# First loads in order of need, products of weights and idle products in TensorE's waits, and a last stage shared over three engines

## The reference

```python
def fp8_gemm_optimized(x, input_scale, kernel, kernel_scale):
    s_in = input_scale[0]
    s_k = kernel_scale[0]
    x_q = (x.astype(jnp.float32) / s_in).astype(jnp.float8_e4m3fn)
    k_q = (kernel.astype(jnp.float32) / s_k).astype(jnp.float8_e4m3fn)
    y = jnp.dot(x_q.astype(jnp.float32), k_q.astype(jnp.float32), preferred_element_type=jnp.float32)
    return y * (s_in * s_k)
...
y = y.astype(dtype) + bias
...
x = _layernorm(x + _L3_ffn_ref(x, L3_ffn_kernel, L3_ffn_input_scale, L3_ffn_kernel_scale, L3_ffn_bias), axis=-1)
```

## Time and profile before

| | |
|---|---|
| median of 3 runs | 1708.81 us (1707.7 to 1712.8) |
| profiled execution | 1693.4 us, span 1691.6 us |
| PE busy | 1276.5 us, 75% of the span |
| DVE busy | 1196.2 us, 71% |
| POOL busy | 811.6 us, 48% |
| ACT busy | 708.3 us, 42% |
| mean granted PE clock | 0.887 |

### The profile page before, as it was taken

One profiled execution on the slowest core, in us unless ns is written; L12 is line 12 of the kernel. 1 busy time (PEld: TensorE's weight loads), 2 busy tenths in 40 slices (PEclk: granted clock), 3 DMA queues, 4 the chain that ended last, 5 costly groups with the idle time before them and its releaser, 6 DMA issues.

```text
span 1691.6 us, 40998 instructions
## 1 busy us (share of the span) xinstructions
PE 1276.5 (75%) x15261; PEld 883.3 (52%) x15261; DVE 1196.2 (71%) x2568; ACT 708.3 (42%) x1453; POOL 811.6 (48%) x1014
## 2 busy tenths in 40 slices
PE   4988868886878868689998786846888742988820
PEld 2555635655645556456665455843555541655510
DVE  3986848994688857578886575435888525997777
ACT  1553425554555544233443353423555420555510
POOL 2553437772376735434552462534566425556610
PEclk9998969998999989789999898877999865999965
DMA  8000000000000000000000000212000102000000
GB/s 326 1 1 1 0 0 1 0 1 22 0 1 0 0 1 13 0 5 1 0 0 1 1 0 26 49 45 106 0 2 0 34 20 21 1 1 1 0 2 25
DMA packets 17814, 29.93 MB, mean 18 GB/s; under 512 B 4211, under 2 KB 14067, under 8 KB 16970
## 3 DMA queue, kind: packets, MB, share of 16 engines
q1 hardware_dynamic: 15818, 24.97, 4.3%
q0 software_dynamic: 1920, 3.94, 1.5%
HBM read 23.91 MB, written 4.98 MB: 17 GB/s over the span
## 4 chain that ended last, share of the span: by engine, by line
PE 40%; DVE 23%; issue 17%; POOL 12%; ACT 5%; DMA 2%; SPq 1%; POOLq 0%; DVEq 0%; ACTq 0%
PE ps L331 31%; DVE maxima L424 6%; PE ps L447 4%; DVE arena L426 4%; PE ps L779 3%; ACT arena L434 2%; DVE heads_out L721 2%; POOL arena L864 2%; POOL arena L511 2%; POOL inv_norm L859 2%; DVE sq_sum L993 1%; POOL rstd L365 1%; POOL arena L1889 1%; DVE gate L1746 1%; POOL arena L2175 1%
## 5 line engine op out<-in xcount | busy, mean ns | idle before, releaser
L331 PE MATMUL ps<-arena 64*64 64x64 f32 (+5 forms) x7937 | 384.7, 280 | 36.2 <-DVE arena L2083 7.0
L331 PEld LDWEIGHTS ps<-arena 64*64 64x64 f32 (+4 forms) x7937 | 238.8, 134 | 166.0 <-issue 121.5
L511 POOL TENSOR_TENSOR arena<-arena,w_const 128x1024 f32<-128x1024 f32 x96 | 182.4, 1901 | 154.8 <-DVE arena L711 68.6
L424 DVE TENSOR_REDUCE maxima<-ps 128x16 f32<-128x1024 f32 (+1 forms) x144 | 158.5, 1101 | 54.6 <-PE ps L331 51.0
L434 ACT ACTIVATE arena<-arena 128x1024 f32<-128x1024 f32 (+1 forms) x144 | 138.5, 962 | 129.3 <-DVE arena L426 128.4
L447 PE MATMUL ps<-w_const,arena 128*128 128x128 f32 x1024 | 145.0, 284 | 50.6 <-ACT arena L434 33.8
L859 POOL TENSOR_TENSOR inv_norm<-sq_floor,minus_half 128x16 f32<-128x16 f32 x32 | 121.9, 3810 | 88.1 <-DVE sq_floor L996 88.0
L426 DVE TENSOR_TENSOR arena<-ps,maxima 128x1024 f32<-128x1024 f32 (+1 forms) x144 | 159.3, 1106 | 4.9
L447 PEld LDWEIGHTS ps<-w_const,arena 128*128 128x128 f32 x1024 | 116.9, 145 | 73.4 <-ACT arena L434 44.0
L441 ACT COPY arena<-ps 128x1024 f32<-128x1024 f32 (+1 forms) x144 | 131.3, 912 | 55.1 <-PE ps L447 55.0
L365 POOL TENSOR_TENSOR rstd<-var_eps,minus_half 128x1 f32<-128x1 f32 x144 | 80.0, 567 | 145.6 <-DVE var_eps L827 101.4
(11 more groups left out here) (296 smaller groups left out, 2663.9 us busy)
## 6 DMA issues: line engine op xcount, KB each, us to landing
experts<-in_pack_moe SPq DMA_DIRECT2D x2, 4180.0 KB, 20.0
w_fa<-in_pack_fa SPq DMA_DIRECT2D x2, 1024.0 KB, 11.8
moe_in<-state SPq DMA_DIRECT2D x2, 1024.0 KB, 5.9
w_a<-in_pack_a SPq DMA_DIRECT2D x1, 1824.0 KB, 16.9
moe_out<-arena SPq DMA_DIRECT2D x5, 256.0 KB, 2.3
w_fg<-in_pack_fg SPq DMA_DIRECT2D x2, 537.0 KB, 12.2
ctxT<-in_ctxT SPq DMA_DIRECT2D x1, 1024.0 KB, 7.8
out<-state SPq DMA_DIRECT2D x1, 1024.0 KB, 5.1
```

Of the source, the lines that this page charges most:

```text
L331: return nc.tensor.matmul(o, lhsT, rhs, start=start, stop=stop, skip_group_check=True)
L424: nc.vector.reduce_max(mx, sc, X_AXIS).then_inc(signal["max_ready"], 1)
L511: nc.gpsimd.tensor_tensor(keys_wide(s).rearrange("p (b h t) -> p b h t", b=SEQS, h=8), key8(s).rearrange("p (b t) -> p b t", b=SEQS).unsqu ...
```

## The change

Six things are done.

- **First loads.** const is cut in a head (identity, causal, own_head, rope8; 328 of 1105 columns) and a rest. SP issues the head, rows, tiles 0 and 1 of x, a0, the other 14 tiles of x, const's rest, and then what came before. DVE's setup makes only what the first stage needs; four tables are made in `late_tables`, behind L0_ATTN. ACT makes one copy of a scratch column before all, and POOL fills the blank values before it waits.
- **Products of weights.** PE makes the biases of a stage, and the chain's 32 products, before it waits for the phase before; the wait until they are kept moves behind the first front. The POOL fill goes behind the first staging.
- **Idle products.** `keep_busy(o, n)` makes n products of 128x512 in bf16 into a bank that nobody reads: 12 before L0_CROSS, 8 and 5 around the chain's wait, 12 before L1_CROSS, 12 and 18 in moe1, 16 before L2_ATTN and before L3_ATTN each (when twelve of the sixteen tiles are done), 12, 10, 10 and 14 in moe2. That is 145.
- **Last stage by three engines.** POOL casts to bf16, adds the bias and the residual and makes the power and the norm's bias. ACT scales the input, squares it, doubles the large values, copies the turned group, scales the output and writes the norm. DVE splits, masks, rounds, takes a row maximum (its way to carry over-range values to NaN) and the statistics. All scratch is double, loops are written out, and the scaling of a later group stands ahead of or behind norms as in the diff.
- **Last stage's loads** are issued after alibi's, long before.
- **Store** of the output by groups, four DMAs of 256 KB.

```diff
+        def keep_busy(o, n):
+            for _ in range(n):
+                mm(o, ident16[:, :], causal16[:, :].unsqueeze(1).broadcast_to([P, 8, S]))
...
-                pool.wait_ge(ctx_loaded, 16)
-                pool.wait_ge(tile_done, 2 + 16 * phases[0])
-                for s in STREAMS:
-                    last = nc.gpsimd.memset(big(s, 4, 8 * 96), 0.0)
-                last.then_inc(values_blank, 1)
+                if phases[0] != L0_ATTN:
+                    pool.wait_ge(ctx_loaded, 16)
+                    pool.wait_ge(tile_done, 2 + 16 * phases[0])
+                def blank_values():
+                    for s in STREAMS:
+                        last = nc.gpsimd.memset(big(s, 4, 8 * 96), 0.0)
+                    last.then_inc(values_blank, 1)
+
+                if phases[0] == L0_ATTN:
+                    blank_values()
...
+                    if front and not middle and front.ph != L0_ATTN:
+                        blank_values()
...
-                pe.wait_ge(tile_done, 2 + 16 * phases[0])
+                bias_bank = bank(1, 3) if phases[0] == L2_ATTN else bank(0, 1)
                 for k, ph in enumerate(phases):
...
-                pe.wait_ge(bias_kept, biases_kept(phases))
+                if phases[0] in (L2_ATTN, L3_ATTN):
+                    pe.wait_ge(tile_done, 2 + 16 * phases[0] - 4)
+                    keep_busy(bank(1, 1) if phases[0] == L2_ATTN else bank(0, 2), 16)
+                elif phases[0] != L0_ATTN:
+                    keep_busy(bank(0, 2), 12)
+                pe.wait_ge(tile_done, 2 + 16 * phases[0])
...
+        def late_tables(dve):
+            dve.wait_ge(const_rest_loaded, 16)
+            dve.wait_ge(loaded["scales"], 16)
+            dve.wait_ge(masks_loaded, 4 * 16)
+            for l in range(2):
+                nc.vector.tensor_tensor(rope_f[l][:, :], part("const", "rope_xpos"),
+                                        weights["scales"][:, l * 256:(l + 1) * 256], ALU.mult)
+            nc.vector.tensor_scalar(own16[:, :], own_u8[:, :], 0.0, OFF, ALU.is_equal, ALU.mult)
...
+                if L0_ATTN in phases:
+                    late_tables(dve)
...
-                pe.wait_ge(tile_done, 2 + 16 * phases[0])
                 for c in range(8):
                     for par in range(2):
                         rows = slice(par * S, (par + 1) * S)
-                        mm(pair(0, 0)[rows, c * D:(c + 1) * D], part("a1", "wv")[rows, c * S:(c + 1) * S],
+                        mm(pair(1, 0)[rows, c * D:(c + 1) * D], part("a1", "wv")[rows, c * S:(c + 1) * S],
                            part("a1", "wo")[rows, c * D:(c + 1) * D])
                 for n, ph in enumerate(GLU):
-                    last = mm(bank(1, 0, n * D, (n + 1) * D), ones_row[:, :], part("rows", glu_pack(ph) + "_b2"))
+                    last = mm(bank(1, 2, n * D, (n + 1) * D), ones_row[:, :], part("rows", glu_pack(ph) + "_b2"))
                 last.then_inc(vo_made, 1)
+                keep_busy(bank(0, 2), 8)
+                pe.wait_ge(tile_done, 2 + 16 * phases[0])
+                keep_busy(bank(0, 2), 5)
                 pe.wait_ge(vo_kept, 1)
                 by_tile_steps(pe, chain_steps(f_tensor(pe), glu_tensor(pe), l1_tensor(pe), phases))
             return run
...
+                keep_busy(bank(0, 2), 12)
...
+            keep_busy(bank(1, 1), 12)
...
+            keep_busy(bank(1, 1), 18)
...
         def fp8_pool(ph):
-            with pool_engine.Fori(0, GROUPS) as g:
-                group_norm_pool(pool_engine, 2, g)
+            pool = pool_engine
+            def bf16_input(g):
+                pool.wait_ge(tile_done, 2 + 16 * (ph - 1) + 4 * (g + 1))
+                if g >= 2:
+                    pool.wait_ge(fs["f_in"], 2 * (g - 2) + 2)
+                nc.gpsimd.tensor_copy(fp[g % 2]["x16"], group_of(state, g)).then_inc(fs["f_x16"], 1)
+
+            for g in range(3):
+                bf16_input(g)
+            for g in range(GROUPS):
+                f = fp[g % 2]
+                pool.wait_ge(fs["f_y16"], g + 1)
+                nc.gpsimd.tensor_tensor(f["sum16"].rearrange("p (t d) -> p t d", t=4),
+                                        f["y16"].rearrange("p (t d) -> p t d", t=4),
+                                        bias8.unsqueeze(1).broadcast_to([P, 4, D]), ALU.add).then_inc(fs["f_biased"], 1)
+                pool.wait_ge(fs["f_biased"], g + 1)
+                if g >= 2:
+                    pool.wait_ge(tile_done, 2 + 16 * ph + 4 * (g - 1))
+                nc.gpsimd.tensor_tensor(f["acc"], group_of(state, g), f["sum16"], ALU.add).then_inc(gs["g_sum"], 1)
+                if g == 0:
+                    bf16_input(3)
+                pool.wait_ge(gs["g_var"], USES + g + 1)
+                nc.gpsimd.tensor_tensor(f["rstd"], f["var"], minus_half[:, 0:4], ALU.pow).then_inc(gs["g_rstd"], 1)
+                pool.wait_ge(gs["g_rstd"], USES + g + 1)
+                nc.gpsimd.tensor_tensor(f["bias"], f["minus_mean"], f["rstd"], ALU.mult).then_inc(fs["f_bias"], 1)
 
         def fp8_tensor(ph):
             pe = tensor_engine
-            turned = ps[0][:, 0, :].bitcast(BF16)
-            with pe.Fori(0, GROUPS) as g:
-                pe.wait_ge(fs["f_rounded"], g + 1)
+            for g in range(GROUPS):
+                f, turned = fp[g % 2], ps[g % 2][:, 0, :].bitcast(BF16)
...
+            def scaled_input(g):
+                f = fp[g % 2]
+                act.wait_ge(fs["f_x16"], g + 1)
+                if g >= 2:
+                    act.wait_ge(fs["f_max"], 2 * (g - 2) + 1)
+                    act.nop(nofuse=True)
+                nc.scalar.activation(f["x"], f["x16"], ACT.Identity, bias=zero8, scale=inv8[:, 0:1])\
+                    .then_inc(fs["f_in"], 1)
+                nc.scalar.activation(f["size"], f["x16"], ACT.Square, bias=zero8, scale=inv8[:, 0:1])\
+                    .then_inc(fs["f_in"], 1)
...
+            for g in range(GROUPS):
+                turned_copy(g)
+                if g == 0:
+                    large_values(1)
+                scaled_output(g)
+                if g >= 1:
+                    normal(g - 1)
+                if g + 2 < GROUPS:
+                    scaled_input(g + 2)
+                if 1 <= g < GROUPS - 1:
+                    large_values(g + 1)
+            normal(GROUPS - 1)
...
+            def round_group(g):
+                f = fp[g % 2]
+                dve.wait_ge(fs["f_in"], 2 * g + 1)
+                half, small = split(f["x"], f["half8"], f["small8"])
+                half.then_inc(fs["f_halved"], 1)
+                small.then_inc(fs["f_masked"], 1)
+                dve.wait_ge(fs["f_in"], 2 * g + 2)
+                nc.vector.tensor_scalar(f["mask"], f["size"], SMALL, None, ALU.is_ge)
+                dve.wait_ge(fs["f_masked"], 2 * g + 1)
+                dve.nop(nofuse=True)
+                if g >= 2:
+                    dve.wait_ge(fs["f_turned"], g - 1)
+                nc.vector.tensor_copy(f["q_x"], f["small8"]).then_inc(fs["f_masked"], 1)
+                nc.vector.reduce_max(f["largest"], f["size"].rearrange("p (t d) -> p t d", t=4), X_AXIS)\
+                    .then_inc(fs["f_max"], 1)
+                dve.wait_ge(fs["f_large"], g + 1)
+                dve.wait_ge(fs["f_masked"], 2 * g + 2)
+                nc.vector.copy_predicated(f["q_x"], f["mask"], f["large"]).then_inc(fs["f_rounded"], 1)
+                dve.wait_ge(fs["f_max"], 2 * g + 1)
+                nc.vector.tensor_scalar(f["over"], f["largest"], OVER, 3e38, ALU.is_gt, ALU.mult)\
+                    .then_inc(fs["f_max"], 1)
+                dve.wait_ge(fs["f_max"], 2 * g + 2)
...
+            head = sum(packs["const"][1][n][1] for n in ("ident", "causal", "own_head", "rope8"))
+            x_tiles = dram["x"].rearrange("(t p) d -> p t d", p=P)
+            sp.dma_start(weights["const"][:, 0:head], packs["const"][0][:, 0:head]).then_inc(loaded["const"], 16)
+            sp.dma_start(weights["rows"][:, :], packs["rows"][0]).then_inc(loaded["rows"], 16)
+            sp.dma_start(state[:, 0:2, :], x_tiles[:, 0:2, :]).then_inc(x_loaded, 16)
             sp.dma_start(weights["a0"][:, :], packs["a0"][0]).then_inc(loaded["a0"], 16)
-            sp.dma_start(state[:, :, :], dram["x"].rearrange("(t p) d -> p t d", p=P)).then_inc(x_loaded, 16)
-            sp.dma_start(weights["rows"][:, :], packs["rows"][0]).then_inc(loaded["rows"], 16)
+            sp.dma_start(state[:, 2:TILES, :], x_tiles[:, 2:TILES, :]).then_inc(x_rest_loaded, 16)
+            sp.dma_start(weights["const"][:, head:], packs["const"][0][:, head:]).then_inc(const_rest_loaded, 16)
             sp.dma_start(weights["scales"][:, :], packs["scales"][0][0].partition_broadcast(P))\
                 .then_inc(loaded["scales"], 16)
 
...
-            sp.wait_ge(tile_done, 2 + 16 * PHASES)
-            sp.dma_start(out.rearrange("(t p) d -> p t d", p=P), state[:, :, :]).then_inc(out_stored, 16)
-            sp.wait_ge(out_stored, 16)
+
```

(7 more changed lines are left out.)

257 lines of the change are left out of this document (147 added, 110 removed).

## The result

The changed kernel takes 1640.23 us (median of 4 runs, 1635.91 to 1646.56) against 1710.8 (median of 4) for the kernel before beside it: ratio 0.9595, 95% interval 0.956 to 0.963, 70.6 us less. The forecast was 1638 in a range of 1623 to 1662.

The account below looks back on a forecast made before the run. No engine holds the whole span (wait chain: PE 40%, DVE 23%, issue 17%). Terms 15.0 + 11.7 + 15.7 + 1.8 − 2.0 + 28.5 = 70.7 us off 1708.8 give 1638.1 us, range 1623 to 1662.

Parts of the forecast that it names:

- Start, 15.0: Start of the kernel: reordered loads and setup bring the first projection from 23.76 to about 8.7 us, saving 15.0 us.
- Rival C: Start: the slow 4.09 us issue of the rows load now delays the first weights; +4 us, 1642; chance 0.07.
- Entries, 11.7: Stage entries: earlier products and fills save 4.8 (chain), 1.6 (L1_CROSS), 2.7 (L2_ATTN) and 2.6 us (L3_ATTN).
- Clock, 15.7 + 1.8 − 2.0: Behind stage borders: idle products raise PE's clock, saving 15.7 us, plus 1.8 in the chain, less 2.0 for overruns.
- expected clock of 0.9 or more: Windows behind borders at L0_CROSS, L1_CROSS, moe1 and moe2: PE's granted clock should read 0.9 or more.
- upper bound of 25.1: Windows behind borders, chain left out: PE's busy time times one minus its clock, at most 25.1 us.
- B: Behind borders: idle products don't hold the clock, or work there isn't bound by PE; 1658 us; chance 0.25.
- Last stage, 28.5: Last stage: early loads, three engines and store by groups end it at 1663.1 against 1691.6, saving 28.5 us.
- the ring: Last stage: a cycle of copy, statistics, power, norm and doubling, put at 6.9 us between copies of groups 2 and 3.
- rival D: Last stage: POOL's adds and DVE's passes take turns, four adds each 0.7 us longer; +3 us, 1641; chance 0.08.
- F: Where PE is dense: added PE work lowers the granted clock, so the kernel gets slower, 1740 at 15%; chance 0.01.
- G: Whole kernel: some older wait keeps each stage where it was; within 0.3% of 1708.8 us; chance 0.01.

Follow-up runs that it names:

- e5_changed_again: The changed kernel with no edit, run again on a chip where the kernel before takes 1693 us: 1620.4 us, ratio 0.9559.
- e2_no_idle_old_entries: Changed kernel without idle products, with biases, chain products and POOL's blank fill back in their old places: 1651.65 us, ratio 0.9764.
- e1_no_idle: The changed kernel without its 145 idle products, all else as it is: 1642.05 us, ratio 0.9702.
- e3_only_last: The kernel before with only the last stage new (three engines, early loads, store by groups): 1663.73 us, ratio 0.9829.
- e4_act_order: The changed kernel with ACT's later input scaling and doubling put ahead of the previous group's norm in the last stage: 1620.06 us, ratio 0.9577.

## Why the prediction was right, point by point

**Total.** 73.8 us on a 1693 chip and 70.6 on a 1710 chip, against 70.7. That the second meets the sum to 0.1 us is luck: single terms missed by up to 2 or 3 us, some up and some down, and the changed kernel's own runs lie 10.7 us apart. The prediction kept the 15.4 us between the profiled execution and the runs as a constant. The runs showed what it was: the chip. It came out right since the changed kernel's first runs were on the slower kind too.

**Start, 15.0.** Right in mechanism, 0.9 low in size: the first projection stood at 7.82 against 8.7, since the weights landed 3.5 us and not 4.1 to 4.6 behind their issue. In e5_changed_again L0_ATTN ends 16.9 earlier. Rival C fell: the issue of the rows took 0.31 us and the first weights were issued at 1.98. "Free" tables were not wholly so: POOL's root and product took 0.58 and 0.77 longer beside them, 0.8 on the path.

**Entries, 11.7.** e2_no_idle_old_entries gives 14.2 without the start (8.5, 1.6, 1.5, 2.6 by stages) against 4.8, 1.6, 2.7 and 2.6. L1_CROSS and L3 are as forecast, and L2_ATTN gave 1.2 less. The chain's entry itself measured 5.2 (the turning is 1.3 us behind the norm's end, and was 6.5); the rest of its 8.5 lies in the chain's spread.

**Clock, 15.7 + 1.8 − 2.0.** Together 15.5, against 21.7 by e1_no_idle, or about 15 once moe1's 6.6 us of luck are set aside, and the pair of before and e5_changed_again agrees with the latter: beyond the entries it gives L1_CROSS 2.5, L2 3.5, moe2 4.8, chain 3.0, moe1 0.7, and −0.4 at L3. Of the single terms L1_CROSS (2.4) was right, L2_ATTN (2.4) and moe2 (4.0) were too low by about 1 and 0.7, and L0_CROSS (3.5, it gained 0.4 to 1.3), moe1 (2.0, it gained 0.7) and L3_ATTN (1.4) too high. The chain's 1.8 is not shown: e1_no_idle lost nothing there. The step that was off in kind is the expected clock of 0.9 or more: in the profile of the changed kernel it was 0.69 to 0.87 at the four places named, and 1.00 only at L1_CROSS in two other profiles. The products hold the clock through the wait but don't keep it from falling a few us on. At L1_CROSS it was 1.00 from 914 to 918 us; PE was busy for 0.32 of the next 2 us, waiting for POOL and DVE, and from 920 it was at the lower level (0.50) while PE was busy without a gap. Cutting the upper bound of 25.1 by more than a third, for which no row stood, was what made the sum right. B fell with e1_no_idle. (The prediction gives the clock behind the borders as 0.50 to 0.71; its rows say 0.50 to 0.69.)

**Last stage, 28.5.** Measured 29.5 by the profiles and 29.7 by e3_only_last. The parts: DVE's first round began at 1608.94 − 1604.5 = 4.4 us behind DVE's last variance where 3.6 was worked out, the ring 6.4 where 6.9 was, and POOL's adds took 1.15 where 1.27 was. From the forecast's list the copies 6.9 us apart came 6.4 apart, and 41.2 us to the end came to 40.2. The groups by form in the stage, of the changed kernel:

```profile
L2482 POOL TENSOR_TENSOR arena<-state,arena 128x512 f32<-128x512 f32 x4 | 4.6, 1151 | 0.3
...
L2515 ACT ACTIVATE arena<-arena,inner 128x512 f32<-128x512 bf16 x4 | 3.2, 803 | 0.1
...
L2585 DVE TENSOR_REDUCE arena<-arena 128x4 f32<-128x512 f32 x4 | 2.7, 677 | 0.0
L2523 ACT ACTIVATE arena<-arena 128x512 bf16<-128x512 fp8e4 x4 | 2.5, 618 | 0.0
```

The row maximum was 0.68 (0.63 taken), ACT's scaling 0.80 (0.6 taken).

**The rule and rival D.** I had written that no row shows POOL and DVE blocking one another. Rows of the changed kernel do: a DVE instruction that takes 0.17 elsewhere ends with POOL's add.

```profile
1614.47 1.15 POOL L2476 TENSOR_TENSOR arena<-arena,inner 128x512 bf16<-128x512 bf16 x1 [5.49 <-ACT arena L2532]
1614.48 1.17 DVE L2594 TENSOR_SCALAR arena<-arena 128x4 f32<-128x4 f32 x1
```

The Trainium skill, page "SBUF — State Buffer", section "SBUF: two separate sides", has the exclusive lock for the whole instruction; these rows and those of e4_act_order agree (0.69 to 1.46, 1.15 to 1.48). It names VectorE's instructions with two SBUF inputs or in a two-port mode; L2594 here has one input, and the trace doesn't tell its mode. The chain's powers agree in one direction alone: behind DVE's product they take 3.91 and not 2.91, but a product that starts behind the power isn't held for the 2.91 us (0.36 at most), so for the power the lock isn't held through the whole instruction. Nor was the trace of the kernel before silent: 30 of its 32 powers take 3.8 or 3.9 us and two take 2.9. The prediction looked at the residual adds, which had no such wait. In the changed kernel it cost next to nothing, since DVE waited for that same add anyway, so D's price of 3 us fell and its mechanism stood.

**F and G.** PE's busy time rose by 26 us with the idle products and the mean granted clock rose from 0.887 to 0.911; F has no support. G fell with the start.

## What to carry to other kernels

Filling an engine's wait with work that is needed anyway (products of weights) took that work off the path (5.2 us at the chain). Filling it with idle products was worth about half of what the windows' busy time times the missing clock says (11 to 12 of 25, the chain left out), and where it was tried only if they ran right up to the real work. Sum the terms stage by stage against a profile from the same chip, and before you call a difference between two profiles a gain, look how far the same stage moves between executions. When work is shared between GpSimd and VectorE, count on their taking turns where they overlap, look in the trace for an instruction whose length has two values (2.91 and 3.91 us here), and give the last group, which nothing can hide, to the engine that waits for it.

## What the runs showed that I had not expected

The same kernel is 17 us slower on some chips, and in the five profiles of the changed kernel and its variants from them moe1 is 15 to 22 us longer: ACT or DVE stand still there, for up to 18 us at a time, with no releaser in the trace, while POOL issues indirect DMAs. It is the same two instructions in all five, ACT's L2060 and DVE's L2154 of the changed kernel. What they wait for was not tried. A chain of 700 us of the same instructions varied from 691.8 to 704.8 with the granted clock, and one added wait in DVE's program, far ahead of it, shortened it to 684.5 to 690.0 by letting POOL's power start first six times.
